# Four graph layers on one core: two transpose banks and a side bank become a ring of three

## The reference

```python
def gat(h, mask, b):                              # layer 1: four heads, then one more (GAT2)
    scores = einsum('nd,md->nm', h, h)
    return softmax(where(mask, scores, -1e16)) @ h + b

def additive(x, W, a, slope):                     # layers 2 and 3 (ADD1, ADD2)
    h = x @ W
    e = leaky_relu((h @ a_left)[:, None] + (h @ a_right)[None, :], slope)
    return softmax(where(mask, e, NEG)) @ h
```

## Time and profile before

| | us |
| --- | --- |
| median of 3 runs (5706.20 to 5715.72) | 5710.56 |
| profiled execution | 5713.95 |
| its span | 5712.2 |
| TensorE busy | 5265.8 |
| VectorE busy | 4372.0 |
| ScalarE busy | 3731.8 |
| POOL busy | 1942.3 |
| mean granted clock of TensorE, share of full speed | 0.978 |

### The profile page before, as it was taken

How to read it: one execution, slowest core, us unless ns; L and a number is a source line. 1 busy time by engine, 2 the same in 40 slices (tenths; PEclk the granted TensorE clock), 3 DMA queues, 4 the chain that set the end, 5 groups by cost and what they waited for, 6 DMA issues and landing times.

```text
span 5712.2 us, 132229 instructions
## 1 busy us (share of the span) xinstructions
PE 5265.8 (92%) x52922; PEld 4508.6 (79%) x52922; DVE 4372.0 (77%) x7325; ACT 3731.8 (65%) x5501; POOL 1942.3 (34%) x1724
## 2 busy tenths in 40 slices
PE   8499999999999899999999999999999999999966
PEld 6388787888878788887878878787888878788755
DVE  5677678778787877778787787878788787877866
ACT  3266557676676757667576666767576675767665
POOL 3400025133341523325241343415233252413466
PEclk9799999999999999999999999999999999999988
DMA  5200000000000000000000000000000000000000
GB/s 177 61 16 11 18 9 9 9 14 14 9 9 11 17 12 7 9 18 12 15 5 10 17 14 9 9 11 16 11 9 9 18 12 15 5 9 18 13 1 5
DMA packets 138241, 95.95 MB, mean 17 GB/s; under 512 B 96032, under 2 KB 115104, under 8 KB 137632
## 3 DMA queue, kind: packets, MB, share of 16 engines
q1 hardware_dynamic: 137632, 87.49, 6.1%
HBM read 35.55 MB, written 8.91 MB: 8 GB/s over the span
## 4 chain that ended last, share of the span: by engine, by line
PE 67%; issue 12%; DVE 6%; POOLq 6%; DVEq 2%; ACT 2%; POOL 1%; DMA 0%; SPq 0%; ACTq 0%
PE po L1067 22%; PE tp L1042 22%; PE pss L1030 9%; PE pss L1031 9%; POOLq L257 6%; DVE pt L1333 3%; DVE rows L1321 2%; PE px L988 2%; DVEq L257 1%; PE px L1055 1%; PE px L1005 1%; ACT rows L1234 1%; PE px L969 1%; PE px L1015 0%; POOL shut L866 0%
## 5 line engine op out<-in xcount | busy, mean ns | idle before, releaser
L1042 PE MATMUL tp<-ident,rows 128*128 128x128 f32 x14336 | 1948.1, 278 | 234.5 <-DVE pt L1333 193.3
L1333 DVE COPY pt<-tp 128x512 f32<-128x512 f32 x2048 | 1332.8, 686 | 921.1 <-PE tp L1042 912.1
L1234 ACT ACTIVATE rows<-rows,nm 128x2048 f32<-128x2048 f32 x896 | 1795.0, 2003 | 323.3 <-DVE nm L1321 321.2
L1042 PEld LDWEIGHTS tp<-ident,rows 128*128 128x128 f32 x14336 | 1600.9, 141 | 476.8 <-issue 308.2
L1067 PE MATMUL po<-pt,hn 128*64 128x128 f32 x28672 | 1782.8, 278 | 37.5 <-ACT ot L1195 36.3
L1067 PEld LDWEIGHTS po<-pt,hn 128*64 128x64 f32 x28672 | 1568.5, 138 | 192.4 <-issue 191.7
L1186 ACT COPY pt<-tp 128x512 f32<-128x512 f32 x1536 | 837.9, 589 | 769.7 <-PE tp L1042 760.9
L869 POOL TENSOR_TENSOR rows<-sr,mask 128x2048 f32<-128x2048 f32 x256 | 1048.7, 4098 | 514.7 <-PE tp L1042 508.4
L1030 PE MATMUL pss<-ha 128*128 128x512 f32 x2560 | 1062.9, 415 | 13.1 <-DMA ha<-hb 12.0
L1031 PE MATMUL pss<-ha,hb 128*128 128x512 f32 x2560 | 1009.5, 394 | 0.0
L1321 DVE CUSTOM_DVE_ANT_0 rows<-pss,mask,nm 128x1024 f32<-128x1024 f32 x640 | 821.7, 1284 | 88.2 <-issue 3.5
(11 more groups left out here) (108 smaller groups left out, 3220.6 us busy)
## 6 DMA issues: line engine op xcount, KB each, us to landing
hb<-ha SPq DMA_DIRECT2D x164, 128.0 KB, 2.3
ha<-hb SPq DMA_DIRECT2D x164, 128.0 KB, 2.3
adjb<-in_adj SPq DMA_DIRECT2D x32, 512.0 KB, 5.6
xin<-x SPq DMA_DIRECT2D x36, 128.0 KB, 2.5
xb<-in_x SPq DMA_DIRECT2D x16, 256.0 KB, 3.0
x<-t SPq DMA_DIRECT2D x16, 256.0 KB, 2.4
xb<-x SPq DMA_DIRECT2D x8, 512.0 KB, 4.0
out<-xb SPq DMA_DIRECT2D x32, 128.0 KB, 1.9
```

What stands on the lines that cost most here:

```text
L1042: last = nc.tensor.transpose(tp[q % 2][:, r * P:(r + 1) * P], rows[:, row.slot, jb * P:(jb + 1) * P], ident[:])
L1234: nc.scalar.activation(rows[:, row.slot, :], rows[:, row.slot, :], ACT.Exp, scale=-1.0, bias=nm[:, row.place, 1:2], accum_out=rs[:, row.pl ...
L1333: nc.vector.tensor_copy(pt[:, CH * q:CH * (q + 1), row.k % SLOTS, :], tp[q % 2][:].rearrange("p (j n) -> p j n", n=P)).then_inc(pt_dve, 1)
```

## The change

The three banks `tp0`, `tp1` and `px` become `ring`, used strictly in turn by whatever comes next in TensorE's program order. `Segment` numbers the uses; ScalarE and VectorE find a tile's bank by its number. A use waits for the copy of the use three before it. The tasks that stood "before" PROLOGUE become a segment of their own, START. For a head, `take_sums` copies `po` into `zt` and waits for neither `out_c` nor `back_c`; POOL multiplies `zt` in place. The core of the diff:

```diff
+        uses = []
+        for s in self.steps:
+            turned = self.row(s - 2)
+            uses += self.side_uses(s)
+            uses += [("turn", turned.k, q) for q in (0, 1) if turned]
+            uses += [("back", r.pair) for r in (self.back(s),) if r]
+            uses += self.side_uses(s + 0.5)
+            uses += [("turn", turned.k, q) for q in (2, 3) if turned]
+        self.use = {key: n for n, key in enumerate(uses)}
...
-        tp = [ctx.enter_context(nc.psum_tensor(f"tp{i}", [P, BANK], F32)) for i in range(2)]
+        ring = [ctx.enter_context(nc.psum_tensor(f"ring{i}", [P, BANK], F32)) for i in range(BANKS)]
         po = ctx.enter_context(nc.psum_tensor("po", [P, BANK], F32))
-        px = ctx.enter_context(nc.psum_tensor("px", [P, BANK], F32))
...
-                    nc.gpsimd.tensor_tensor(dst, ot[:], ob[:].rearrange("p r n -> p (r n)"), ALU.mult)
+                    nc.gpsimd.tensor_tensor(dst, dst, ob[:].rearrange("p r n -> p (r n)"), ALU.mult)
...
+            def take(*key):
+                n = taken[0]
+                taken[0] += 1
+                if freed[n % BANKS]:
+                    pe.wait_ge(*freed[n % BANKS])
+                return ring[n % BANKS]
+            def give(count, n):
+                freed[(taken[0] - 1) % BANKS] = count.sem, n
...
             def turn(row, q):
 
-                if q >= 2:
-                    wait_copy(row, q - 2)
-                elif row.before:
-                    wait_copy(row.before, q + 2)
+                tile = take("turn", row.k, q)
                 for r in range(CH):
                     jb = CH * q + r
-                    last = nc.tensor.transpose(tp[q % 2][:, r * P:(r + 1) * P],
+                    last = nc.tensor.transpose(tile[:, r * P:(r + 1) * P],
                                                rows[:, row.slot, jb * P:(jb + 1) * P], ident[:])
                 last.then_inc(tr_ready, 1)
+                count = copied[row.copier[q]]
+                give(count, count.n + row.count[q] + 1)
...
-                px_free()
-                nc.tensor.transpose(px[:, 0:P], turned, ident[:]).then_inc(back_ready, 1)
-                px_used(back_c)
+                tile = take("back", row.pair)
+                nc.tensor.transpose(tile[:, 0:P], turned, ident[:]).then_inc(back_ready, 1)
+                handed(back_c)
...
             def take_sums(row):
 
+                wait(pv_c, pv_c.n + row.pair + 1)
+                if row.unit < H:
+                    nc.scalar.copy(zt[:, row.unit, row.t // 2, :], po[:, 0:P]).then_inc(ot_ready, 1)
+                    return
                 if row.pair or back_c.n:
-                    used = out_c if where[0].behind_head(row) else back_c
-                    wait(used, used.n + row.pair)
-                wait(pv_c, pv_c.n + row.pair + 1)
+                    wait(back_c, back_c.n + row.pair)
                 nc.scalar.copy(ot[:], po[:, 0:P]).then_inc(ot_ready, 1)
```

More of the change, by code:

```diff
@@ L53 @@
 RING = 4
+BANKS = 3
+SIDE = ("xn", "xt", "proj", "hn", "h", "r")
 PROJ = {GAT2: 0, 0: 1, 1: 0, 2: 1, 3: 0}
@@ L104, in __init__ @@
         blocks = [r for r in self.rows if r]
-        for before, row in zip([None] + blocks, blocks):
-            row.slot_user, row.before = row.k - RING, before
+        for row in blocks:
+            row.slot_user = row.k - RING
         own = [r for r in blocks if r.k < self.blocks]
@@ L115, in __init__, with side_uses @@
             self.tasks.setdefault(step, []).append((name, unit, c))
-        assert all(k == "before" or int(k) in self.steps for k in self.tasks), self.tasks.keys()
+        assert all(int(k) in self.steps for k in self.tasks), self.tasks.keys()
+        uses = []
[7 more added lines that the diff above has]
+        self.use = {key: n for n, key in enumerate(uses)}
+        assert len(self.use) == len(uses)
+    def side_uses(self, key):
+        return [task for task in self.tasks.get(key, []) if task[0] in SIDE]
     def tasks_at(self, step):
@@ L126, in odd @@
         return row if row and row.odd else None
-    def behind_head(self, row):
-        earlier = [r for r in self.rows if r and r.k == row.k - 2]
-        return earlier[0].unit < H if earlier else False
     def back(self, step):
@@ L141, in sequence @@
     def sequence(self):
-        return [(s, *task) for s in sorted(k for k in self.tasks if k != "before") for task in self.tasks[s]]
+        return [(s, *task) for s in sorted(self.tasks) for task in self.tasks[s]]
     def tally(self, *names):
@@ L162, in prologue @@
     order = [pair for u, hn in ((0, 1), (1, 2), (2, 1), (3, 2)) for pair in pairs_of(u, hn)] + [None] * GAP
-    tasks = [("before", "xn", 0, c) for c in range(NC)]
-    tasks += [("before", name, 0, g) for g in range(2) for name in ("proj", "low", "hn")]
+    tasks = []
     for u in range(H - 1):
@@ L173, in prologue, with start @@
     return Segment(order, False, True, tasks)
+def start():
+    tasks = [(0, "xn", 0, c) for c in range(NC)]
+    return Segment([], False, False, tasks + [(0, name, 0, g) for g in range(2) for name in ("proj", "low", "hn")])
 def next_head(first):
@@ L233, in epilogue @@
     return Segment(order, True, False, tasks)
-PROLOGUE, LOOP, EPILOGUE = prologue(), main_loop(), epilogue()
+START, PROLOGUE, LOOP, EPILOGUE = start(), prologue(), main_loop(), epilogue()
 class Count:
@@ L247, in run_segments @@
 def run_segments(run):
+    run(START)
     run(PROLOGUE)
@@ L935, in _ @@
             rc_c = Count(rc_ready)
-            px_copied = [None]
+            taken, freed, where = [0], [None] * BANKS, [None]
             def wait(count, n=None):
@@ L944, in wait_copy, with handed @@
                 wait(count, count.n + row.count[q] + 1)
[L946 to L950, removed]
+            def take(*key):
+                n = taken[0]
+                assert where[0][0].use[key] + where[0][1] == n, key
+                taken[0] += 1
[4 more added lines that the diff above has]
+                freed[(taken[0] - 1) % BANKS] = count.sem, n
+            def handed(count):
                 count.n += 1
-                px_copied[0] = count
+                give(count, count.n)
             def run_task(name, unit, c):
@@ L956, in run_task @@
                 if name == "xn":
-                    px_free()
+                    px = take(name, unit, c)
                     xin_c[c % 2].n += 16
@@ L962, in run_task @@
                     last.then_inc(xn_psum, 1)
-                    px_used(xn_c)
+                    handed(xn_c)
                 elif name == "xt":
-                    px_free()
+                    px = take(name, unit, c)
                     xr_c.n += 1
@@ L970, in run_task @@
                     last.then_inc(xt_psum, 1)
-                    px_used(xt_c)
+                    handed(xt_c)
                 elif name == "proj":
-                    px_free()
+                    px = take(name, unit, c)
                     if unit == GAT2:
@@ L990, in run_task @@
                     last.then_inc(proj_psum, 1)
-                    px_used(hc_c)
+                    handed(hc_c)
                     halves_c.n += 64
                 elif name == "hn":
-                    px_free()
+                    px = take(name, unit, c)
                     wait(hc_c)
@@ L999, in run_task @@
                     last.then_inc(hn_psum, 1)
-                    px_used(hn_c)
+                    handed(hn_c)
                 elif name == "h":
-                    px_free()
+                    px = take(name, unit, c)
                     wait(xt_c)
@@ L1017, in run_task @@
                     last.then_inc(right_psum, 1)
-                    px_used(sr_c)
+                    handed(sr_c)
             def dot_products(row):
@@ L1073, in run_segment @@
             def run_segment(segment):
-                for task in segment.tasks.get("before", ()):
-                    run_task(*task)
+                where[0] = segment, taken[0]
                 for s in segment.steps:
@@ L1134, in next_of, with tile_of @@
                 wait(count)
+            where, used = [None], [0]
+            def tile_of(*key):
+                return ring[(used[0] + where[0].use[key]) % BANKS]
             def run_task(name, unit, c):
@@ L1138, in run_task @@
                 blocks = slice(c * CH, (c + 1) * CH)
+                px = tile_of(name, unit, c) if name in SIDE else None
                 if name == "xn":
@@ L1172, in run_task @@
                     nc.scalar.mul(sr[:, cols], px[:], SLOPES[unit]).then_inc(sr_ready, 1)
-            where = [None]
             def hn_of(unit):
-                return [r.hn for r in where[0].rows if r and r.unit == unit][0]
+                rows_of = where[0].rows if where[0].blocks else PROLOGUE.rows
+                return [r.hn for r in rows_of if r and r.unit == unit][0]
             def copy_tile(row, q):
@@ L1186, in copy_tile @@
                 nc.scalar.copy(pt[:, CH * q:CH * (q + 1), row.k % SLOTS, :],
```

(15 more changed lines are left out.)

## The result

The changed kernel takes 6000.15 us (median of 4, 5998.11 to 6004.85) against 5712.09: ratio 1.0507, 95% interval 1.0488 to 1.0525. Slower as forecast, but by 288 us instead of 133, and outside the range (5785 to 5885).

What follows compares the result with a forecast made beforehand. The prediction took TensorE, busy 92% of the span, to bound the kernel. Its terms, 126 + 17 + 7 - 10 - 3 - 4 = +133 us on the profiled execution, gave 5847, forecast as 5843 us for the median; range 5785 to 5885.

Steps and rivals of the forecast that it cites:

- The edge: LOOP's mixed stretch: t0 after a step with a back waits for take_back behind the exp; 2.49 us later at step 37.
- the tail: LOOP's steps 101 to 111: late t0 starts mostly fall into idle time; 2.5 us a LOOP, +17 us, bounds 0 and 57.
- The gap of 0.51 at step 36: Mixed stretch: 0.51 us of t0's idle time that the ring frees, claimed to give nothing.
- the forecast's terms for its eight places: LOOP's delayed t0 starts, nine in all: 16.7 us a LOOP, 18.0 with 0.14 us per release; +126 us over seven LOOPs.
- EPILOGUE: Additive rows after LOOP: the same wait seven times, 1.0 us in ADD1, somewhat more in ADD2; +7 us, bounds 0 and 12.
- TensorE's busy time stays near 5266: Sign in the profile after: TensorE's busy time in us unchanged, its share falling to 90%.
- rival 3: Mixed stretch: stalls lower TensorE's granted clock, 33 us a LOOP, 230 us more, 6073 us; chance 0.04.
- Rival 1: Transposes' waits: the extra bank makes the kernel faster, 5668 us, or 5521 if all waits on L1333 went; chance 0.06.
- `proj` and `hn` no longer wait for `sr`: Side tasks at steps 21 and 29, twice a LOOP: three banks remove 4.8 us in all for each line; -10 us.
- t0 doesn't wait for `ob` among the head rows of LOOP: Between head rows: eight dot products cover the same wait with 0.84 us to spare; no cost.
- `zt` is worth nothing: Heads' sums copied straight into `zt`: ScalarE's wait for POOL goes, mattering only in the tail; -4 us, bounds 0 and -36.
- LOOP's period: Sign in the profile after: one LOOP takes 17 to 20 us longer.

Runs made afterwards that it cites:

- The edge alone: Kernel before, old banks untouched, with one wait more: group 0 of the next step waits for take_back at the ring's places; 6014.06 us, 1.0516.

## Why the prediction was half right

*The edge.* Right in mechanism, place and size. t0 behind a back waits for `take_back` behind the exp, at nine steps of LOOP and in the tail; 2.49 us forecast at step 37, 2.49 measured. The gap of 0.51 at step 36 is gone and gave nothing, as argued: from t0 of step 33 to t0 of 37 the changed kernel takes 24.78 us, where it was 20.79, so 3.99 more, and these are the 2.49 of the wait and the 1.5 that the clock costs there. The edge alone makes the loss, and moving its copy takes it away.

*All waiting together.* 133 us forecast, 157 us more of idle time measured. In the mixed stretch the forecast's terms for its eight places come to 16.7 - 1.86 + 8 x 0.14 = 16.0 us, and the idle time grew by 16.3. The tail was mis-sized: 2.5 us a LOOP forecast, 5.1 measured. (A sixth wait for `ob` stands there, at step 107: t0 waited 2.10 us for VectorE before and waits 2.15 for `ob` now.) EPILOGUE was +7; its trace has ten waits for `ob` instead of seven, but from the first t0 of its ADD1 rows to the end of the span it took 231.8 us against 232.4, so it cost nothing.

*The clock.* Here the prediction failed. The sum has no term for it, and "TensorE's busy time stays near 5266" was to be the sign; it is 5393.1. The step that failed is the dismissal of rival 3, at a chance of 0.04: "against it, the tail has such short stalls now and shows 0.98, and the new mixed stretch would look like that, 147.6 busy of some 176". The new mixed stretch shows 0.92. The stalls of the old tail were 0.5 to 2.1 us, the new ones 2.1 to 3.5, and a stretch's mean says nothing of a single gap: behind the longest of those in the old tail, 2.10 us before 3309.46, the clock was 0.57 from 3310.46 to 3313.46. A row of the evidence hinted at it too: behind a wait of 1.80 us, eight transposes took 1.89 us, where they take 1.16 behind 0.51. In the changed kernel it is 1.43 - 1.16 for the transposes and 3.22 - 1.97 for the sums, 1.5 us at step 37. The rival's own price, 230 us, was too high, its chance far too low; the forecast needed it as a second term, not as another case.

But that term couldn't have been read off one row, for not every gap has such a stretch behind it. Two places of the kernel before with the same wait of 1.80 us, and one of the changed kernel behind a wait of 3.22 us:

```profile
2935.35:2938.35 3.00, 3.00 (x20) 2.67 (x22) 2.87 (x5) 2.23 (x5) 1.06 (x2) 0.51 0.00 0
2981.43:2984.43 3.00, 3.00 (x41) 2.54 (x41) 2.87 (x5) 2.04 (x5) 1.06 (x2) 1.00 0.02 5
```

```profile
3089.80:3095.80 6.00, 6.00 (x59) 5.27 (x60) 2.61 (x6) 3.22 (x5) 1.00 (x2) 1.00 0.00 0
```

In that LOOP of the changed kernel 11 of the 15 places are followed by some us at a clock of 0.50, the lower level of 1.2 GHz, and four are not. What decides it stays open. Over all 114 places the 127 us of added busy time are 1.1 us a place.

The Trainium skill, TensorE: Matmul & The Clock Gate, section A second HAM failure mode, tells of a clock that goes up and down from short idles while cycling through PSUM banks. By kind that is what this trace shows: mean clock 0.948 against 0.979 with the idles filled. Here the idles came from one late reader and not from the cycling: the old banks with the edge alone show 0.949 too, and the ring with an early reader holds 0.979.

*Rival 1.* The rotation of banks that the Trainium skill, Perfetto Trace Analysis, section Matmuls, advises does gain here, 68 us, but only with the late reader of the ring made prompt. That "it decides if `ob` is ready within 1.7 us of the back" was the right condition: moved between the lifts, the copy ends 0.69 us after the back starts.

*The rest.* `proj` and `hn` no longer wait for `sr`, t0 doesn't wait for `ob` among the head rows of LOOP, and `zt` is worth nothing. LOOP's period, read between the waits for `hn` of two LOOPs, grew by 37.1 us (672.8 before, from 2762.62 to 3435.45; 709.9 now, from 2878.72 to 3588.61), where 17 to 20 were to be the sign.

## What to carry to other kernels

A ring shared in program order makes each user wait for the slowest reader of the tile three before it, so price it by the latest copy, not by the mean; then move that copy ahead of the long instruction it stands behind. When a change lengthens a wait of TensorE, add what the matmuls behind it may cost at the lower clock: look in the old trace for the longest gaps already there, and compare the granted clock and the matmuls' durations behind all of them with the usual ones, since some gaps here were followed by slow matmuls and others of the same length were not.

## What I had not expected of the hardware

Nearly half of the loss (127 of 288 us by TensorE's busy time) is TensorE slower behind gaps of 2 to 3.5 us, in a stretch where it is busy 179.9 of 209.1 us. Zero products in those gaps bring the clock back and make the changed kernel 147 us faster, though they add nothing to the result; the earlier copy, at 5635, makes them needless. At step 37 the granted clock still reads 1.00 in the gap and falls only in the matmuls behind it (0.70, then 0.59).
